# The fourth tile's output projection moves from a bank of scores to a bank of turned probabilities

## The reference

```python
scores = einsum('bqhd,bkhd->bhqk', sq, sk) * scale
attn = softmax(where(causal, scores, min), axis=-1)
y = einsum('bhqk,bkhd->bqhd', attn, sv)
o = 0.5 * y + 0.5 * o_gla          # o_gla: the gated linear attention
x = x + o.reshape(b, n, H * D) @ Wo   # H * D = 2048, n = 512
```

## Time and profile before

| what | value |
|---|---|
| time, median of 3 runs | 2868.56 us (2867.84 to 2871.44) |
| the profiled execution: time | 2872.15 us |
| the profiled execution: span of its instructions | 2869.7 us |
| PE busy | 2592.1 us, 90% |
| DVE busy | 1936.6 us, 67% |
| ACT busy | 1554.0 us, 54% |
| POOL busy | 1549.3 us, 54% |

### The profile page before, as it was taken

The page is one execution under the profiler, slowest core; times in us unless marked ns, Lnnn a source line. Parts: engine busy times, 40 slices in busy tenths (PEclk is TensorE's granted clock), DMA queues, the critical chain, the costliest instruction groups (busy, mean ns, idle before and its releaser), DMA issues. The chain is left out here.

```text
span 2869.7 us, 52448 instructions
## 1 busy us (share of the span) xinstructions
PE 2592.1 (90%) x16740; PEld 1703.5 (59%) x16740; DVE 1936.6 (67%) x4731; ACT 1554.0 (54%) x4655; POOL 1549.3 (54%) x1623
## 2 busy tenths in 40 slices
PE   3899999999999999999999999999984899979882
PEld 2566666666666666666666666666653444447661
DVE  5677667677776776777677767767754777747661
ACT  4566556655655555666566555656543333237661
POOL 3556445655655564566556545655520566646663
PEclk9899999999999999999999999999996999989996
DMA  4500000000000000000000000000002222339985
GB/s 169 186 1 16 1 30 1 16 30 1 1 16 31 1 16 28 3 1 16 30 1 2 15 31 1 1 31 1 1 1 107 94 69 68 132 117 272 265 231 147
DMA packets 65355, 156.78 MB, mean 55 GB/s; under 512 B 13367, under 2 KB 14647, under 8 KB 64256
## 3 DMA queue, kind: packets, MB, share of 16 engines
q1 hardware_dynamic: 48624, 132.91, 13.6%
q0 software_dynamic: 16384, 16.33, 3.1%
q10 hardware_dynamic: 80, 4.19, 0.4%
HBM read 120.31 MB, written 81.40 MB: 70 GB/s over the span
## 5 line engine op out<-in xcount | busy, mean ns | idle before, releaser
L403 ACT ACTIVATE prob<-score_ps,neg_max 128x512 f32<-128x512 f32 (+3 forms) x512 | 271.8, 531 | 308.1 <-DVE neg_max L566 278.6
L280 POOL TENSOR_TENSOR parts<-qk,rope 128x640 f32<-128x640 f32 x128 | 197.0, 1539 | 383.1 <-issue 326.2
L793 PE MATMUL out_ps<-prob_t,val 128*128 128x512 f32 (+3 forms) x1024 | 302.3, 438 | 14.0 <-ACT prob_t L409 13.1
L768 PE MATMUL score_ps<-kr_t,qr_t 128*128 128x512 f16 (+3 forms) x1536 | 284.7, 300 | 13.0 <-ACT prob L403 11.2
L574 DVE TENSOR_SCALAR prob<-prob,inv_sum 128x512 f32<-128x512 f32 (+3 forms) x512 | 273.7, 535 | 18.0
L793 PEld LDWEIGHTS out_ps<-prob_t,val 128*128 128x128 f32 x1024 | 185.4, 191 | 127.6 <-issue 62.1
L445 ACT ACTIVATE soft<-qk,neg_top 128x128 f32<-128x128 f32 x640 | 247.1, 387 | 5.5 <-DVE neg_top L588 2.1
L566 DVE TENSOR_REDUCE neg_max<-score_ps 128x1 f32<-128x512 f32 (+3 forms) x512 | 237.4, 483 | 7.1 <-PE score_ps L770 0.9
L309 POOL TENSOR_TENSOR decay<-keys 128x512 f32<-128x512 f32 x128 | 134.0, 1047 | 167.0 <-DVE keys L616 167.0
L835 PE MATMUL qkv_ps<-wq_high,x_t_high 128*128 128x512 f16 x512 | 195.8, 382 | 15.8 <-DVE wkv_low L514 15.8
L318 POOL TENSOR_TENSOR k_dec<-decay,keys 128x512 f32<-128x512 f32 x128 | 163.0, 1273 | 68.7 <-ACT decay L461 68.7
(11 more groups left out here) (267 smaller groups left out, 7701.0 us busy)
## 6 DMA issues: line engine op xcount, KB each, us to landing
held_expert_w<-in_L_ffn_W_gate_dram SPq DMA_DIRECT2D x32, 512.0 KB
held_expert_w<-in_L_ffn_W_up_dram SPq DMA_DIRECT2D x32, 512.0 KB
held_expert_w<-in_L_ffn_W_down_dram SPq DMA_DIRECT2D x32, 512.0 KB, 7.7
rows<-const_empty_dram SPq DMA_DIRECT2D x1, 10560.0 KB, 38.8
e_xg<-rows SPq DMA_DIRECT2D x32, 330.0 KB
x_in<-_attn_hidden_states_dram SPq DMA_DIRECT2D x8, 1024.0 KB, 5.5
x_acc<-_attn_hidden_states_dram SPq DMA_DIRECT2D x8, 1024.0 KB, 5.5
x<-x_acc SPq DMA_DIRECT2D x8, 1024.0 KB, 4.4
```

Source lines behind the costliest of these rows:

```text
L280: nc.gpsimd.tensor_tensor(parts[:, 1, :].rearrange("p (h d) -> p h d", d=HALF), qk[:].rearrange("p (h d) -> p h d", d=HALF), rope[:, i, 1: ...
L403: nc.scalar.activation(prob[:, i % 2, 0:w], score_ps[i % 2][:, 0:w], ACT.Exp, bias=neg_max[:, j:j + 1], accum_out=row_sum[:, j:j + 1]).the ...
L768: nc.tensor.matmul(score_ps[i % 2][:, 0:w], qr_t[p][:, q_, h, i * P:(i + 1) * P], kr_t[p][:, k_, 0:w], start=(n == 0), stop=False)
L793: nc.tensor.matmul(out_ps[:, j * P:SEQ], val[p][:, j, :], prob_t[:, j, j * P:SEQ], start=(j == 0), stop=False, skip_group_check=True)
```

## The change

Tile 3's projection goes into `prob_ps[1]`, for `project_first`, `project_last` and `residual` alike. With it four waits change:
- `project_first` of tile 3 no longer waits for `x2_added[1]` (tile 1's residual) and `exp_ready[1]`, but for `past_copied` and `diag_ready`, the two copies out of `prob_ps[1]` for the unit's last head.
- `scores` of an odd tile waits for one residual fewer: tile 1's of the unit before, no longer tile 3's.
- `turn_probs` of tile 3 for a unit's first head waits for `x2_added[1]` at its full count, which is tile 3's residual of the unit before.
- In the first unit of all, odd `scores` have no wait for `x2_added[1]`.

```diff
--- before.py
+++ after.py
@@ -176,6 +176,10 @@
 
 
         PROJECTION = (0, 1, 3, 2)
+
+        def projection_ps(i):
+
+            return prob_ps[1] if i == NT - 1 else score_ps[i % 2]
         ALL_LOADS = 16 * 5
 
 
@@ -660,7 +664,7 @@
                         dve.wait_ge(x2_added[i % 2], NT // 2 * c)
                     else:
                         dve.wait_ge(acc_loaded, 16 * (b + 1))
-                    nc.vector.scalar_tensor_tensor(out=x_acc[:, i, :], in0=(bank or score_ps[i % 2])[:],
+                    nc.vector.scalar_tensor_tensor(out=x_acc[:, i, :], in0=(bank or projection_ps(i))[:],
                                                    scalar=0.5 / (O_SCALE * W_SCALE), in1=x_acc[:, i, :], op0=ALU.mult,
                                                    op1=ALU.add).then_inc(x2_added[i % 2], 1)
 
@@ -762,8 +766,10 @@
                 pe.wait_ge(exp_ready[i % 2], k)
                 if g and i % 2 == 0:
                     pe.wait_ge(x2_added[0], NT // 2 * c - 1)
-                else:
-                    pe.wait_ge(x2_added[i % 2], NT // 2 * c)
+                elif i % 2 == 0:
+                    pe.wait_ge(x2_added[0], NT // 2 * c)
+                elif c:
+                    pe.wait_ge(x2_added[1], NT // 2 * c - 1)
                 for n, (q_, k_) in enumerate(THREE):
                     nc.tensor.matmul(score_ps[i % 2][:, 0:w], qr_t[p][:, q_, h, i * P:(i + 1) * P], kr_t[p][:, k_, 0:w],
                                      start=(n == 0), stop=False)
@@ -773,6 +779,8 @@
             def turn_probs(c, h, i):
                 n = block_index(c, h, i)
                 pe.wait_ge(prob_ready, n + 1)
+                if i == NT - 1 and h == 0:
+                    pe.wait_ge(x2_added[1], NT // 2 * c)
                 if i == 2:
                     pe.wait_ge(o_whole_ready, G * c + h)
                 else:
@@ -802,18 +810,22 @@
 
                 for i in tiles:
                     pe.wait_ge(o_t_ready, G * (c + 1) - 1)
-                    pe.wait_ge(exp_ready[i % 2], G * NT // 2 * (c + 1))
-                    pe.wait_ge(x2_added[i % 2], NT // 2 * c + i // 2)
+                    if i == NT - 1:
+                        pe.wait_ge(past_copied, (NT - 1) * G * (c + 1))
+                        pe.wait_ge(diag_ready, NT * G * (c + 1))
+                    else:
+                        pe.wait_ge(exp_ready[i % 2], G * NT // 2 * (c + 1))
+                        pe.wait_ge(x2_added[i % 2], NT // 2 * c + i // 2)
                     for h in range(G - 1):
                         for m, (o, w) in enumerate(THREE):
-                            nc.tensor.matmul(score_ps[i % 2][:], o_t[o][:, h, i * P:(i + 1) * P], wo[w][:, G * g + h, :],
+                            nc.tensor.matmul(projection_ps(i)[:], o_t[o][:, h, i * P:(i + 1) * P], wo[w][:, G * g + h, :],
                                              start=(h == 0 and m == 0), stop=False)
 
             def project_last(c, g, tiles):
                 for i in tiles:
                     pe.wait_ge(o_t_ready, G * (c + 1))
                     for m, (o, w) in enumerate(THREE):
-                        ins = nc.tensor.matmul(score_ps[i % 2][:], o_t[o][:, G - 1, i * P:(i + 1) * P],
+                        ins = nc.tensor.matmul(projection_ps(i)[:], o_t[o][:, G - 1, i * P:(i + 1) * P],
                                                wo[w][:, G * g + G - 1, :], start=False, stop=(m == 2))
                     ins.then_inc(projected, 1)
```

## The result

| kernel | median us | lowest to highest | runs |
|---|---|---|---|
| before | 2870.0 | 2867.84 to 2874.26 | 4 |
| changed | 2849.27 | 2847.72 to 2853.43 | 4 |

The ratio is 0.9926, with a 95% interval of 0.991 to 0.9942: faster by 16.6 to 25.8 us, 21 in the middle. The forecast was 2848.7 us, 19.9 us less. The profiled execution took 2849.18 us, with a span of 2846.7, against 2869.7 before.

What follows compares the result with a forecast made beforehand. The prediction took PE, through its waits in the attention, to bound the kernel. It summed 18.9 + 1.05 = 19.9 us less, taken from the median 2868.56 us, to a forecast of 2848.7 us, range 2844.5 to 2857.

Steps and rivals of the forecast that it cites:

- What bounds the kernel: In the attention PE is busy 1956.26 of 2019.00 us, so time is lost only where PE waits or works slower.
- What the stall costs: Tile 3's first projection matmul waits for tile 1's residual: 0.61 us from start to start, 18.9 us in 31 units.
- rival 1: At tile 3's projection, part of the stall comes back at once: gain only 14.5 us, 2854.1 us; chance 0.10.
- The last unit: No transposes precede tile 3's projection there; the removed wait is worth 1.05 us.
- The waits put in, and those dropped, cost and give nothing: New waits at tile 3's projection and first transposes (5.6 us of cover), and the scores' dropped wait: all nothing.
- rival 3: The wait moves to the next unit's first transposes: 9.3 us slower, 2877.9 us; chance 0.02.
- `chunk_local` next: PE reaches `chunk_local` 0.61 us sooner, still 1.0 us behind the later of its inputs from POOL and DVE.
- Tile 3's residual from another bank: DVE's residual of tile 3 changes length by at most 0.05 us either way, and is not on PE's path.
- Nothing is given back inside the unit: DVE, ACT and POOL idle at the boundary, so all shift earlier together and PE's later waits keep their size.
- Rival 2: The stall moves to PE's waits inside the unit, taking up 19.9 us: 2868.6, no change; chance 0.08, in part or full.
- No fall of the clock in the attention: From 124 us on the granted clock is full, 2.4 GHz; removing idle gives no reason for a fall.
- The time itself: Whole kernel: 2848.7 us, a full gain of some 20 us; chance 0.80.

Runs made afterwards that it cites:

- experiment 1: Changed kernel with tile 3's first projection matmul again waiting for tile 1's residual, though it writes the other bank: 2871.75 us, ratio 1.0006.
- experiment 2: Kernel before with DVE taking tile 1's residual behind the two products of `apply_decays` instead of ahead of them: 2944.43 us, ratio 1.0257.
- experiment 3: Changed kernel with DVE taking tile 1's residual behind the two products of `apply_decays`: 2852.06 us, ratio 0.9932.
- Experiment 6: Changed kernel with tile 2's projection of a sequence's last unit held over into the next sequence's first unit: 2830.46 us, ratio 0.9861.
- experiment 4: Changed kernel with the next unit's odd scores again waiting for tile 3's residual: 2853.16 us, ratio 0.9937.
- experiment 5: Changed kernel with tile 3's residual moved on DVE behind the next unit's two normalisations, at 24 boundaries inside sequences: 2858.21 us, ratio 0.995.
- experiment 7: Changed kernel with `gate_logs` and `soften_keys` taken by DVE ahead of the second normalisation: 2905.51 us, ratio 1.012.
- experiment 8: Changed kernel with tile 2's projection held across sequences and the soft keys taken ahead of the second normalisation: 2881.32 us, ratio 1.0029.

## Why the prediction was right

- *What bounds the kernel*: PE in the attention, and there its waits. Experiments 1 to 3 moved one wait of PE alone, and the time followed. Experiment 6 moved PE's own work into its waits, with the same outcome.
- *What the stall costs*: 0.61 us from the starts, against 0.44 from the modelled ends. Measured 0.60 (1.039 to 0.437). Between the first and the last of the 31 boundaries, 30 units, it was 1944.56 us before and is 1928.66 now; with the two falls of 1.24 us taken off, 18.4 us are gone, 0.61 a unit. 0.44 a unit would have given 13.2. With the 0.60 of the first boundary and the 1.0 behind the last, these two profiles give 20.0 us for the change, against 19.9 forecast. The rule of the Trainium skill that decided this (Perfetto Trace Analysis, section Tensor Engine Instruction (MATMUL, LD_WEIGHTS)) holds here, and rival 1 is out.
- *The last unit*: 1.05 us forecast, 1.26 - 0.21 = 1.05 measured.
- *The waits put in, and those dropped, cost and give nothing*: no entry for them in the waits (`attend` with the same two counts stands six calls ahead, not the two that I wrote, which only helps); experiment 4 for the scores, experiment 5 for the transposes, whose 5.6 us of cover were real. In rival 3, though, the price was put at 31 boundaries. Experiment 5 made its condition true at 24 and paid at 8 of them: at the others the normalisations are done early enough for the residual to fit in.
- *`chunk_local` next*: 1.0 us of cover forecast, 1.03 left.
- *Tile 3's residual from another bank*: 691 ns in the middle of 32, as from the old bank.
- *Nothing is given back inside the unit*: the remaining waits kept their sizes. Rival 2 is out. I had said that the second and the last boundary would come 17.7 us closer; it is 1880.45 - (2085.91 - 220.75) = 15.3. The 2.4 missing are the two falls of the clock.
- *No fall of the clock in the attention*: the argument, that the change only takes idle out, was right about the change and wrong about the stretch. The first profile of the kernel before happened to show none; its second has one, and the two of the changed kernel have two each.
- *The time itself*: the forecast came within 0.6 us of the median, and that close it is luck. It started from a median of 2868.56 us for the kernel before, which with the fourth run is 2870.0. The stretch behind the attention differs by up to 4.8 us between profiles, the falls take up to 4 us, and the interval of the gain is 16.6 to 25.8 us. What the runs bear out is the 20 us by the starts, and that all of it goes with the wait (experiment 1).

## What to carry to other kernels

- Two uses of one bank make a chain: fill, read, fill. Look for a bank that is idle just there. If all waits that the new bank needs are already behind the engine, and the released reader has slack before its own next waiter, the whole stall is won.
- A wait is worth its full length only if no other engine carries work over it. Read the idle of all of them just behind the stall. Where they all wait for the stalled engine, everything shifts; where one has no slack (as DVE in experiment 7), a wait that is removed comes back.
- Another order on one engine also changes what its work runs beside. Look up what each moved instruction costs in its new company, as `gate_logs` in experiment 7.
- Take a PE stall from start to start, against the same step where it waits for nothing.

## What the runs showed of the hardware that was not expected

- PE's granted clock falls from 2.4 to 1.2 GHz in the middle of a stretch in which PE is 97% busy (the changed kernel's attention). Ahead of such falls PE stood for 0.56, 0.67 and 1.03 us one after the other (first units), for 0.45, 0.59 and 1.05 us one after the other (the last unit), or for 2.17 us at once (experiment 2) and once for 2.95 us (experiment 5). It does not fall each time: 0 to 3 times in a profile for the eight profiles with the kernels' own gaps (before and changed twice each, experiments 1, 3, 4 and 7), 5 times in experiment 5, 11 times with 2.17 us in each unit, and not once in the two profiles in which the first units' gaps were filled (6 and 8). A fall made its unit 0.9 to 1.7 us longer: 0.9 in experiment 7, 1.2 in the first units of the others, 1.5 and 1.7 in the last unit (experiment 4 and the changed kernel's second profile), 1.6 to 1.7 in experiment 2.
- How long a DVE instruction takes depended on what POOL did beside it. The normalisation of 128 x 384 values took 0.42 us with no POOL instruction beside it, 0.83 to 0.84 beside the rotation of 128 x 320 (93 times in each of the two kernels), and 1.00 beside the multiplication of 128 x 512 (experiment 7). `gate_logs` of 128 x 128 took 0.28 us alone and 0.95 beside the rotation (medians of the changed kernel and of experiment 7).
